# Where TensorE's increments stand in the two edge loops: on the last product, or on a drain behind it

## What is computed

```
h = relu(layernorm(x))
# layer 0: 8 heads of 16
q, k, v = (h @ Wq)[dst], (h @ Wk)[src], (h @ Wv)[src]
att  = exp(clip(sum over a head of q*k, -10, 10))
res0 = segment_sum(att * v, dst) / (segment_sum(att, dst) + 1e-8)
x = x + (layernorm(res0 + h) * gamma + beta)
# layer 1: cosine attention with a softmax over each node's edges
h = relu(layernorm(x))
alpha = cos_beta * dot(h[dst], h[src]) / (|h[dst]| * |h[src]|)
w = exp(alpha - segment_max(alpha, dst))
x = x + segment_sum(w * h[src], dst) / segment_sum(w, dst)
```

## Time and profile before

| | |
|---|---|
| median of the timed runs | 5060.37 us |
| the profiled execution, its span | 7130.1 us |
| PE matmul busy | 4342.2 us (61%) |
| VectorE busy | 4103.2 us (58%) |
| GpSimd busy | 3380.1 us (47%) |
| ScalarE busy | 2444.7 us (34%) |
| mean granted TensorE clock | 0.683 |

### The profile page before, as it was taken

How to read it: one execution, slowest core, us unless ns; L and a number is a source line. 1 busy time by engine, 2 the same in 40 slices (tenths; PEclk the granted TensorE clock), 3 DMA queues, 4 the chain that set the end, 5 groups by cost and what they waited for, 6 DMA issues and landing times. The chain is left out here.

```text
span 7130.1 us, 118004 instructions
## 1 busy us (share of the span) xinstructions
PE 4342.2 (61%) x22945; PEld 3749.1 (53%) x22946; DVE 4103.2 (58%) x12176; ACT 2444.7 (34%) x8557; POOL 3380.1 (47%) x3426
## 2 busy tenths in 40 slices
PE   6997555555555555555455156677667676666665
PEld 3886344434443444434344156676666676666665
DVE  8998555555555555555556545555555555555555
ACT  4997111111110111111011544454454444444443
POOL 1334555545454554545454245555555555555552
PEclk8998666666666666666666576666676666776666
DMA  1001222222222222222222112121221121112111
GB/s 35 25 23 34 81 80 76 77 75 77 74 79 77 77 77 75 77 75 79 77 76 73 38 43 48 46 48 47 48 47 47 47 49 46 47 47 49 46 45 39
DMA packets 211652, 414.52 MB, mean 58 GB/s; under 512 B 69399, under 2 KB 103640, under 8 KB 211068
## 3 DMA queue, kind: packets, MB, share of 16 engines
q0 software_dynamic: 135184, 326.41, 17.4%
q1 hardware_dynamic: 74048, 79.04, 3.8%
q10 hardware_dynamic: 1836, 4.03, 0.2%
HBM read 363.52 MB, written 42.48 MB: 57 GB/s over the span
## 5 line engine op out<-in xcount | busy, mean ns | idle before, releaser
L892 POOL DMA_INDIRECT kv_rows<-kv_table,idx_ring x1643 | 1624.6, 989 | 1590.9 <-issue 1003.7
L892 POOL DMA_INDIRECT h_rows<-h_table,idx_ring x1652 | 1566.7, 948 | 1592.7 <-issue 1029.9
L1132 PE MATMUL psum<-vx,hot 128*128 128x136 f32 x3336 | 864.0, 411 | 1135.6 <-DVE acc L1165 1041.0
L1132 PEld LDWEIGHTS psum<-vx,hot 128*128 128x128 f32 x3336 | 696.2, 287 | 1280.3 <-DVE acc L1165 1140.8
L1628 DVE SCALAR_TENSOR_TENSOR h_sb<-h_sb,corr,psum 128x129 f32 x1668 | 582.8, 349 | 931.8 <-PE psum L1586 496.4
L1165 DVE TENSOR_TENSOR acc<-acc,psum 128x136 f32 x1668 | 489.4, 293 | 1006.2 <-remote 850.0
L1576 PE MATMUL psum<-ident,hotl 128*128 128x128 f32 x1668 | 393.9, 381 | 952.7 <-DVE highs L1654 880.6
L1080 ACT ACTIVATE vx<-clip 128x32 f32<-128x32 f32 x417 | 95.2, 229 | 2332.1 <-DVE clip L1209 1878.7
L1576 PEld LDWEIGHTS psum<-ident,hotl 128*128 128x128 f32 x1668 | 258.5, 192 | 1030.6 <-issue 895.4
L1121 PE MATMUL psum<-q_sb,hotT 128*128 x3336 | 712.0, 380 | 32.9 <-issue 23.0
L1121 PEld LDWEIGHTS psum<-q_sb,hotT 128*128 128x128 f32 x3336 | 607.5, 273 | 184.7 <-issue 184.7
(11 more groups left out here) (225 smaller groups left out, 5834.1 us busy)
## 6 DMA issues: line engine op xcount, KB each, us to landing
hand<-kv_table SPq DMA_DIRECT2D x3200, 1.0 KB
hand<-h_table SPq DMA_DIRECT2D x2048, 0.5 KB
own_rows<-own SPq DMA_DIRECT2D x104, 256.0 KB
own<-own_rows SPq DMA_DIRECT2D x104, 256.0 KB
h_rows<-h_table,idx_ring POOLq DMA_INDIRECT x1652
kv_rows<-kv_table,idx_ring POOLq DMA_INDIRECT x1643
kv_table<-kv SPq DMA_DIRECT2D x21, 256.0 KB, 2.1
out<-q_sb SPq DMA_DIRECT2D x2, 1536.0 KB
```

The source lines that it names most:

```text
L892: pool.indirect_dma_start(out=G[:, k, j, :], out_offset=None, in_=table, in_offset=bass.IndirectOffsetOnAxis(ap=idx[:, k, j:j + 1], axis=0 ...
L1132: last = nc.tensor.matmul(S_ps[j // HALF][:, j % HALF, :], hot[:, k, j * P:(j + 1) * P], vx[:, k, j, :], start=True, stop=True)
```

## The change

After each set of products in the two loops the increment is taken off the last matmul and put on a drain instruction of TensorE that is issued behind the set. That is three drains in each group of layer 0 (`B`, `Q`, `S`) and four in each group of layer 1 (`Q`, `L`, `S`, `E`). Nothing else changes: the same products in the same order, the same waits, the same values of the semaphores.

```diff
@@ spread_row
-    nc.tensor.matmul(out, pick_row[:, g_u % FOUR, :], rows[:, h, :], start=True, stop=True).then_inc(s_spread, 1)
+    nc.tensor.matmul(out, pick_row[:, g_u % FOUR, :], rows[:, h, :], start=True, stop=True)
+    nc.tensor.drain().then_inc(s_spread, 1)
@@ layer0_edges, TensorE's step
                         last = nc.tensor.matmul(Q_ps[k][:, j * P:(j + 1) * P], hotT[:, k, j * P:(j + 1) * P],
...
-                    last.then_inc(s_q, 1)
+                    nc.tensor.drain().then_inc(s_q, 1)
...
-                    last.then_inc(s_sum, 1)
+                    nc.tensor.drain().then_inc(s_sum, 1)
@@ layer1_edges, TensorE's step
-                    last.then_inc(s_q, 1)
+                    nc.tensor.drain().then_inc(s_q, 1)
...
-                    last.then_inc(s_L, 1)
+                    nc.tensor.drain().then_inc(s_L, 1)
...
-                    last.then_inc(s_sum, 1)
+                    nc.tensor.drain().then_inc(s_sum, 1)
...
-                    last.then_inc(s_E, 1)
+                    nc.tensor.drain().then_inc(s_E, 1)
```

More of the change, by code:

```diff
@@ L1575, in step @@
                     for j in range(GT):
-                        last = nc.tensor.transpose(L_ps[u % 2][:, j * P:(j + 1) * P],
+                        nc.tensor.transpose(L_ps[u % 2][:, j * P:(j + 1) * P],
                                                    hotl[:, (u - 2) % TRIO, j * P:(j + 1) * P], ident[:, :])
-                    last.then_inc(s_L, 1)
+                    nc.tensor.drain().then_inc(s_L, 1)
                 if inside(i - 8):
```

## The result

The kernel with drains takes 6531.87 us (median of three, 6508.95 to 6560.73) where the kernel before took 5060.37: 1.291 times as long, 95% interval 1.288 to 1.294. The forecast was 6160 us with a range up to 6500, so the direction and most of the size were right and the range was missed by 32 us.

The account below looks back on a forecast made before the run. POOL's gathers were taken to pace both loops. To the timed 5060 us it added 75 for layer 0 and 1026 for layer 1, mostly at half clock: 6160 us; forecast's own range 5700 to 6500, whole range 5150 to 6500.

Parts of the forecast that it names:

- What bounds the kernel before: Both loops: POOL's gathers set the pace, 4.92 us a group in layer 0 and 4.95 in layer 1.
- the stops: Long waits in the profile of the kernel before, its span 2070 us longer than timed; taken for the profiler's.
- 5038: Model of the kernel before: 4119 us of POOL's gathers plus 919 us outside them, against 5060 timed.
- The hole: Behind each drained set, between sets that touched before: 0.5 us at full clock, 0.55 at half.
- Layer 1 at the full clock: Layer 1's group grows from a 4.22 us ring to 5.27 us, 0.32 over POOL's 4.95: +133 us.
- the clock stays up: Rival B: layer 1 stays at full clock, +133 us, layer 0 adds 0 to 75; 5190 to 5270 us, chance 0.25.
- Which clock?: Layer 1: four fifths of the time at half clock, 7.41 us a group, +1026 us.
- always half in layer 1 alone: Top of the forecast's range, 6500 us: layer 1 at 8.26 us a group throughout, +1380 us.
- address arithmetic: TensorE's sequencer work queued behind the drain; about 0.2 us for two waits or register operations before the next weight load.
- +75 us for layer 0: Layer 0 with three holes a group, half the time at each clock: 5.10 us a group against 4.92.
- The expected signs: PE timeline: holes of about 0.5 us behind every set, no sets touching, layer 1's mean clock at or under 0.62.
- 0.68 or more: Sign of a wrong prediction: layer 1's mean clock stays at 0.68 or rises.

Follow-up runs that it names:

- the extra product: Kernel before, without drains, plus one extra bf16 product of 512 columns behind layer 1's `Q` set: 5062.02 us, ratio 1.000.
- the single drain behind `Q`: Kernel after with only layer 1's drain behind `Q` kept, all other drains taken back: 5068.85 us, ratio 1.001.
- the missing loads: Kernel before with TensorE's block numbers loaded once ahead of each loop, not once in four groups (wrong blocks' queries in `Q`): 5065.31 us, ratio 1.0005.
- drains alone: Kernel after with layer 0's drains taken back, so drains in layer 1 only (`Q`, `L`, `S`, `E`): 6413.25 us, ratio 1.268.
- the free drain: Kernel after with increments back on the last product and a drain without an increment behind every set in both loops: 6381.03 us, ratio 1.262.
- the counting one: The kernel after, whose drains carry the increments in both loops, against the kernel before: 6531.87 us, 1.291 times as long.

## Why the prediction missed

*What bounds the kernel before* was right: POOL's gathers in both loops (the extra product, the single drain behind `Q` and the missing loads leave 5060 within 7 us), and the stops as the profiler's. That 5038 came so near 5060 was in part luck, for two errors cancel: the gathers take 4183 us and not 4119, and what lies outside them 878 us and not 919.

*The hole.* Forecast 0.55 us at half the clock. The four holes of the group shown make 2.11 us, 0.53 each, and the group takes 8.17 us (forecast 8.26). Right.

*Layer 1 at the full clock.* Forecast 5.27 us a group, +133 us. The trace with drains alone has groups of 5.11 us, which would be +63. With the clock held up by extra products and without the loads it is +149 in all, 136 of them between the first and last gather (2206 us against 2070), but that has the extra products in it. So the forecast was of the right size and rather high, and the rival "the clock stays up" did not happen.

*Which clock?* This is the step that failed. "I take four fifths of layer 1's time at half" was a choice, and the trace says 0.94. The direction was right: the share rose from 0.24. At 8.26 and 5.27 us a group the prediction's own formula gives 1 / (0.94 / 8.26 + 0.06 / 5.27) = 7.99 with that share, (7.99 - 4.95) x 417 = +1266 where it had +1026. That is 240 of the 372 us that were missing. The range had no room for it: its top of 6500 was "always half in layer 1 alone", and 5060 + 1380 with the forecast's own 75 for layer 0 is already 6515. The prediction also read that the clock rose where PE had been busy without a break. With drains it rises now and then without that: at 4523.64 above a set is still at half (1.08 us), and the next one, behind a hole, is at full.

*The loads.* The prediction named "address arithmetic" behind the drain and priced two short operations; it did not look at what else TensorE's sequencer does in front of `Q`. The load of 1.1 us once in four groups is what the forecast left out: 102 us in layer 0, where it is nearly the whole loss, and in layer 1 424, where its own length is some 142. Put at nothing, it is also the greater part of the wrong share: without the loads 0.82 of layer 1's time is at half, nearly the four fifths, and the two loops' losses are 26 and 927 us. That would make some 6015 us, inside the range and below the forecast. The forecast's +75 us for layer 0 were near the measured 97 to 128 by luck, for they were put on groups at half the clock, and the clock there moved only from 0.73 to 0.71 or 0.72.

*The expected signs*: no two sets of layer 1 that touch, layer 1's mean clock under 0.62, layer 0 with the small share of the loss: all seen. The sign "0.68 or more" for being wrong was set by the profile with the stops; undisturbed traces without drains there have 0.88.

What stays open: why the share of time at half rises so steeply between one drain (0.28 at most) and four (0.92 to 0.94). The runs give the steps, not a law; and how the 151 us between the free drain and the counting one divide between later readers and the clock was not tried.

## What to carry to other kernels

Put an increment on the last product, not on a drain behind it: the drain holds TensorE's sequencer, so what was prepared under the running set moves into the open. Here a register load of 1.1 us, once in four groups, cost more than the drains' own holes in layer 0 (102 against 26 us). Before pricing such a stop, list every instruction that the sequencer issues between two sets, the rare ones of a period of several groups too. And where the time at the low clock is longer than the pace of the engine that bounds, small holes can cost many times what they cost with the clock up (here, without the loads, 927 us against 149), so price both levels and let the range reach to all of the time at the low one.

## What the runs showed of the hardware

- Extra matmuls can make a kernel faster. 1668 bf16 products of 512 columns took a loop from 3380 to 2439 us between its first and last gather by raising the mean clock from 0.54 to 0.91.
- Short holes between sets go with a low clock. At half the clock a group with four drains needs 8.2 us, at full 5.1, and layer 1 was at half for 0.92 to 0.94 of its time with four drains a group, 0.24 without. That the wider spread of the same products keeps the low level up was argued and not shown.
- A second drain right behind the first lasts 13 ns in the trace and costs 0.09 us of the kernel's time.
- A profiled execution can be 41% longer than a timed one (7130 against 5060 us) with long stops in all sequencers, and the next profile of nearly the same kernel shows none of them.
